# Cross-attention on one core: both blocks of scores in one run, the output product one round later, second-stage pieces behind the projections

## The reference, cut to what matters

```python
# layer 0, attention: 8 heads of 64, keys and values from the context (77 rows) and from the tokens themselves
xn, cn = layer_norm(x, ln_x_w, ln_x_b), layer_norm(ctx, ln_l_w, ln_l_b)
q = xn @ Wq
k, v = split(concat(xn, cn) @ Wkv)
q, k = l2norm(q) * q_scale, l2norm(k) * k_scale
p = softmax(8.0 * q @ k.T + mask)
x = x + layer_norm((p @ v) @ Wo, ln_o_w, ln_o_b)
# layer 0, feed-forward: a quantised product; layer 1: attention through We and W2, then one expert of 8 per token
```

## Time and profile before

| | |
|---|---|
| three timed runs | 951.37, 953.4, 954.11 us; median 953.4 |
| profiled execution, its own time | the profile gives its span, 950.6 us, and no other figure |
| TensorE busy | 912.8 us (96% of the span) |
| VectorE busy | 744.9 us (78%) |
| ScalarE busy | 693.5 us (73%) |
| GpSimd busy | 458.1 us (48%) |
| TensorE's granted clock, mean | 0.997 |
| most time on the chain that ended last | TensorE 69%, VectorE 14%, ScalarE 8% |

### The profile page before, as it was taken

One profiled execution on the slowest core, in us unless ns is written; L12 is line 12 of the kernel. 1 busy time (PEld: TensorE's weight loads), 2 busy tenths in 40 slices (PEclk: granted clock), 3 DMA queues, 4 the chain that ended last, 5 costly groups with the idle time before them and its releaser, 6 DMA issues.

```text
span 950.6 us, 30821 instructions
## 1 busy us (share of the span) xinstructions
PE 912.8 (96%) x11286; PEld 794.5 (84%) x11286; DVE 744.9 (78%) x2526; ACT 693.5 (73%) x1671; POOL 458.1 (48%) x1094
## 2 busy tenths in 40 slices
PE   7999999999999999999999999999999999899997
PEld 6788888788878887888788878888888878898997
DVE  5566787888888888888888888888888978877553
ACT  4877777677778787778777777777778766676664
POOL 5422433354535453545354444444454545777554
PEclk9999999999999999999999999999999999999999
DMA  7743000000000000000000000000000022245310
GB/s 196 200 124 57 2 2 2 2 13 2 14 2 14 2 14 2 13 3 10 5 10 5 8 8 8 7 8 7 8 8 8 7 47 71 61 97 106 95 55 20
DMA packets 45193, 31.44 MB, mean 33 GB/s; under 512 B 11555, under 2 KB 40166, under 8 KB 45046
## 3 DMA queue, kind: packets, MB, share of 16 engines
q1 hardware_dynamic: 39398, 19.93, 9.2%
q0 software_dynamic: 4320, 8.50, 2.8%
q10 hardware_dynamic: 1328, 1.06, 0.4%
HBM read 17.75 MB, written 12.17 MB: 31 GB/s over the span
## 4 chain that ended last, share of the span: by engine, by line
PE 69%; DVE 14%; ACT 8%; issue 3%; POOL 3%; DMA 1%; SPq 1%; DVEq 0%; POOLq 0%; ACTq 0%
PE ps L1670 9%; PE ps L1717 9%; PE ps L1643 7%; PE ps L1765 6%; PE ps L1450 5%; PE ps L1622 5%; PE ps L1630 5%; PE ps L1452 5%; PE ps L1451 5%; DVE sumsq L1267 4%; PE ps L1722 3%; ACT probs L604 2%; PE ps L1749 2%; ACT qk_hat L617 2%; PE ps L1496 1%
## 5 line engine op out<-in xcount | busy, mean ns | idle before, releaser
L1374 DVE TENSOR_TENSOR qk_hat<-ps,rstd 128x512 f32<-128x512 f32 x168 | 106.3, 684 | 49.2 <-POOL rstd L870 49.1
L1267 DVE TENSOR_REDUCE sumsq<-qk_hat 128x8 f32<-128x512 f32 x168 | 107.8, 677 | 35.9 <-ACT qk_hat L617 34.7
L863 POOL TENSOR_TENSOR rs_t<-rs_y 128x32 f32<-128x32 f32 x73 | 17.9, 245 | 235.2 <-ACT rs_y L658 235.2
L1670 PE MATMUL ps<-v_x,prob 128*64 128x65 f32 x2048 | 127.9, 225 | 2.1 <-ACT w_all L568 0.4
L1670 PE MATMUL ps<-v_c,prob 128*64 128x65 f32 x2048 | 124.2, 222 | 0.0
L677 ACT ACTIVATE prob<-ps,neg_shift 128x512 f32<-128x512 f32 x128 | 88.4, 690 | 48.6 <-PE ps L1717 48.6
L1670 PEld LDWEIGHTS ps<-v_x,prob 128*64 128x64 f32 x2048 | 105.0, 137 | 20.9 <-issue 19.2
L617 ACT ACTIVATE qk_hat<-ps 128x512 f32<-128x512 f32 x168 | 98.5, 599 | 31.7 <-PE ps L1452 25.8
L1450 PE MATMUL ps<-w_hi,xc_hi 128*128 128x512 f32 x272 | 120.8, 444 | 0.8 <-POOL xc_lo L835 0.8
L1717 PE MATMUL ps<-qT_all,kT_all 64*128 64x128 f32 x1536 | 111.6, 285 | 2.3 <-ACT prob L677 1.1
L1452 PE MATMUL ps<-w_hi,xc_lo 128*128 128x512 f32 x272 | 107.3, 395 | 0.0
(11 more groups left out here) (245 smaller groups left out, 2257.2 us busy)
## 6 DMA issues: line engine op xcount, KB each, us to landing
x_res<-sorted_rows SPq DMA_DIRECT2D x71, 65.5 KB, 1.9
w_all<-in_L_ffn_W_dram SPq DMA_DIRECT2D x16, 256.0 KB, 5.3
sorted_rows<-fill SPq DMA_DIRECT2D x8, 327.5 KB
out_dram<-prob,x_res POOLq DMA_INDIRECT x71
sorted_rows<-stage,idx POOLq DMA_INDIRECT x64, 2.4
ctx_res<-in_ctx_dram SPq DMA_DIRECT2D x8, 115.5 KB
x_res<-in_x_dram SPq DMA_DIRECT2D x1, 768.0 KB
sorted_rows<-fill SPq DMA_DIRECT2D x1, 524.0 KB, 5.0
```

The lines of the kernel that those rows point to most:

```text
L1267: nc.vector.reduce_sum(sumsq[:, n * H:(n + 1) * H], sq[:, n * INNER:(n + 1) * INNER].rearrange("p (h d) -> p h d", d=DH), AX).then_inc(ss_ ...
L1374: nc.vector.tensor_tensor(qk_hat[:, n * INNER:(n + 1) * INNER].rearrange("p (h d) -> p h d", d=DH), ps_qk[:, n, :].rearrange("p (h d) -> p ...
L1670: last = nc.tensor.matmul(dst[half:half + DH, :], prob[:, kt, col + half:col + half + DH], v, start=kt == 0, stop=kt == 1)
```

## The change

The numbers of instructions and their shapes stay as they are. The two blocks of scores follow one another directly; the second waits for on_done, since quarters 2 and 3 now use banks 4 and 3. The transposed output goes to bank 6 and waits for the exp that reads it. The output product of batch j - 2 stands behind the first transposes of round j, and waits for o_t. slot_a waits for the first three exps. In rounds of rho 1, 2 and 3 slot_b stands behind the query and key products, and the quantised transposes behind all of them. In slot_c of rho 0 the transposes of t_b stand ahead of the rank matmuls. ScalarE does exps 0 and 1, the scaled tokens, exp 3, o_t, exp 2, and copies the quantised transposes after all squares. VectorE takes the statistics of the next tokens ahead of those of ps_o; the reciprocal of the second stage's sums ahead of the sums of squares; `places` behind them; and `later` behind o_n.

```diff
-        ps_v, ps_ot = (ps[:, 6, :], ps[:, 5, :]), ps[:, 3, :]
-        ps_s = (ps[:, 6, :], ps[:, 5, :], ps[:, 4, :], ps[:, 6, :])
+        ps_v = (ps[:, 6, :], ps[:, 5, :])
+        ps_s = (ps[:, 6, :], ps[:, 5, :], ps[:, 4, :], ps[:, 3, :])
...
+        def output_bank(j, inside):
+
+            return ps[:, 6, :] if has(j, inside) else ps[:, 3, :]
...
-                        if n == 0:
-                            quantised_copied()
+                    quantised_copied()
...
-                if has(j, inside):
-                    exps((0,))
                 if not inside and j == 0:
                     second_weights(j)
+                if has(j, inside):
+                    exps((0, 1))
                 if inside or j != -2:
                     scaled_tokens()
+                if has(j, inside):
+                    exps((3,))
                 if has(j - 1, inside) and not tail(j, inside):
                     outputs_copied()
                 if has(j, inside):
-                    exps((1, 3, 2))
+                    exps((2,))
...
+            def sums_inverted(j, rho, g, inside):
+                if rho == 1 and group(g - 1, inside):
+
+                    after(dve, "pr_done", g - 1, inside)
+                    nc.vector.reciprocal(sinv[0:M, :], ssum[0:M, :]).then_inc(s["sinv_done"], 1)
...
-                if has(j - 2, inside):
-                    dve.wait_ge(wo_done, j - 1)
-                    nc.vector.bn_stats(o6[:, :], ps_o).then_inc(o_bn, 1)
-                    dve.wait_ge(o_bn, j - 1)
-
...
                 if has(j - 2, inside):
+                    dve.wait_ge(wo_done, j - 1)
+                    nc.vector.bn_stats(o6[:, :], ps_o).then_inc(o_bn, 1)
...
                 if not tail(j, inside):
-                    places(j, rho, g, inside)
+                    sums_inverted(j, rho, g, inside)
                 if not inside and TOTAL_AT <= j < TAIL:
                     first_table(j, 0)
                 if has(j + 1, inside) and (inside or j != -1):
                     sums_of_squares(j, pos)
-
                 if not tail(j, inside):
-                    later(j, par, rho, g, inside)
+                    places(j, rho, g, inside)
...
+                if not tail(j, inside):
+                    later(j, par, rho, g, inside)
...
             def slot_a(j, rho, g, inside):
 
+                if has(j - 1, inside):
+                    pe.wait_ge(exp_done, 4 * j - 1)
...
+            def outputs(b, inside):
+
+                pe.wait_ge(ot_done, b + 1)
+                if has(b + 3, inside):
+                    pe.wait_ge(xct_sb, b + 4)
+                elif has(b - 1, inside):
+                    pe.wait_ge(o_cent, b)
+                for t in range(PAIRS):
+                    last = nc.tensor.matmul(ps_o, o_t[:, t * P:(t + 1) * P], wo_sb[:, t, :],
+                                            start=t == 0, stop=t == PAIRS - 1)
+                last.then_inc(wo_done, 1)
...
+                if has(j - 2, inside) and (inside or j <= B):
+                    outputs(j - 2, inside)
                 slot_a(j, rho, g, inside)
...
-                slot_b(j, rho, g, inside)
+                between = rho == 0 or not has(j + 1, inside)
+                if between:
+                    slot_b(j, rho, g, inside)
...
-                        if n == 0:
-                            quantised(j, rho, g, inside)
-                else:
-                    quantised(j, rho, g, inside)
+                quantised(j, rho, g, inside)
+                if not between:
+                    slot_b(j, rho, g, inside)
                 slot_c(j, rho, g, inside)
...
                     scores(0)
+                    if has(j - 1, inside):
+                        pe.wait_ge(on_done, j)
...
+                    scores(1)
...
                     pe.wait_ge(on_done, j)
+                    if has(j, inside):
+                        pe.wait_ge(exp_done, 4 * j + 1)
...
-                if has(j, inside):
-
-                    pe.wait_ge(exp_done, 4 * j + 1)
-                    if halves(pos)[0] != halves(pos)[1]:
-                        pe.sem_inc(s["fence_t"], 1)
-                    scores(1)
-                if has(j - 1, inside):
-
-                    pe.wait_ge(ot_done, j)
-                    if not has(j + 2, inside) and has(j - 2, inside):
-                        pe.wait_ge(o_cent, j - 1)
-                    if has(j + 2, inside):
-                        pe.wait_ge(xct_sb, j + 3)
-                    for t in range(PAIRS):
-                        last = nc.tensor.matmul(ps_o, o_t[:, t * P:(t + 1) * P], wo_sb[:, t, :],
-                                                start=t == 0, stop=t == PAIRS - 1)
-                    last.then_inc(wo_done, 1)
+                if has(j - 1, inside) and not has(j, inside):
+                    outputs(j - 1, inside)
```

## The result

The changed kernel takes 956.8 us (median of 6 runs, 954.6 to 959.0) against 953.0 us (median of 6, 951.4 to 954.1): a ratio of 1.0041 with a 95% interval of 1.0027 to 1.0056. It is slower by 0.4%. The prediction said 946.9 us and faster; the time lies inside its range of 935 to 958, on the wrong side of the kernel before.

The account below looks back on a forecast made before the run. TensorE was taken as the clock. Scores to slot +0.86 us and slot to scores -1.85 made -1.0 us per eight-round period, -6.5 us over 6.5 periods: 946.9 us from a median of 953.4, range 935 to 958.

Parts of the forecast that it names:

- B: Round with two token blocks transposed, two tiles next; first score matmul to first matmul after next transposes: 5.08 to 5.50 us.
- Part 1: Joining both score blocks on TensorE saves tile changes: about 0.38 us a round, half that in four rounds a period.
- Part 2: Second score block waits for o_n, starting 1.11 us after the scores began; restarting costs 0.06 us.
- Part 3: Output product waits for o_t, late in ScalarE's queue: TensorE stands 0.8 us in B, 0.37 in C.
- A: Round with one token block transposed, three tiles next; scores to slot forecast 5.04 us, from 5.32 (-0.28).
- C: Round with two token blocks transposed, three tiles next; scores to slot forecast 5.50 us, from 5.43 (+0.07).
- Part 4: Transposes at L1643 come 1.3 us earlier; qk_hat mostly ready, D gains 0.31 us, one round a period loses 0.6.
- D: Round with one token block, three tiles and a late o_n; scores to slot forecast 5.28 us, from 5.59 (-0.31).
- Part 5: Slot to scores, the rest of a round: moved pieces cover waits for o_c, onehot and tc_t, -1.85 us a period.
- Drains that pay in full: Rival: o_t comes early, so all saved tile-change drains count: 918 us, halfway about 932; chance 0.15 for both.
- Nothing lands: Rival: TensorE reaches the scores earlier but waits the same time for qk_hat, period unchanged: 953 us; chance 0.14.
- VectorE's head: Rival: late statistics of ps_o at VectorE's start of the round delay everything behind, 0.3 us a round: 960 us; chance 0.16.

Follow-up runs that it names:

- e1: The changed kernel with one swap in ScalarE's queue, o_t copied ahead of the exp of quarter 3: 941.0 us.
- e8: The changed kernel without joined scores (banks, waits and exps' order as before); later output product, moved pieces and statistics' order stay: 939.1 us.
- e4: The changed kernel with places alone moved back ahead of the sums of squares on VectorE: 952.5 us.
- e3: The kernel before with only the second-stage pieces moved as in the change, on TensorE, ScalarE and VectorE: 937.2 us.
- e2: The changed kernel with the second-stage pieces back at their old places; joined scores and later output product stay: 973.8 us.
- e9: The changed kernel with o_t copied ahead of the exp of quarter 3 and places ahead of the sums of squares: 939.9 us.
- e10: The kernel before with the second-stage pieces moved and places ahead of the sums of squares: 932.0 us.
- e11: e9 with the token transposes, and their wait for bank 7, between the two blocks of scores: 936.8 us.
- e7: The changed kernel with later (and the table's second pieces) behind the scaled tokens and the residual on VectorE: 967.3 us.
- e12: e8 with VectorE's statistics of ps_o at the head of the round, waiting there for the later output product: 949.3 us.

## Why the prediction was wrong

**Its sign turned on sizes, added over a period.** The mechanism, waits for o_n and o_t that give the drains back, was named rightly. The step that failed is the sum of the first part, scores to slot: 0.86 us a period was forecast and 1.81 measured, 0.67 of the difference in the three B rounds (1.26 forecast, 1.93 measured). Two smaller steps failed beside it: the prediction had nobody waiting for place, and rounds 59 to 62 were counted as rounds like the others. Of its parts:

*Part 1* was right in its price of a change of tile, and there is no break between the blocks but the one of part 2.

*Part 2* placed the second block at 1.11 us after the first; the record of 2.27 us agrees. The term that was too small is the restart. I took 0.06 us from transposes, since the block stays in one mode. It is 0.10 us, as on a change of mode, for scores and for the output product (the first records after a wait are 373 and 377 ns long, as at a drain). With two stalls in most rounds that is an estimated 0.08 us a round.

*Part 3* named the wait that gave the gain back, and its mechanism is shown by e1 (15.8 us from one swap) and e8 (17.7 us without the joined scores). Its sum was too small: A 5.14 (5.04 predicted), B 5.73, 5.63 and 5.63 (5.50), C 5.60 twice (5.50). In the first B a mode entry for L1501 was left out. The "before" of B was also taken from one round, 5.08; the other two stood at 4.99, which hides another 0.18 us a period. (The round of the earlier trace rows errs the other way: it stood at 5.42, not at A's 5.32.) In all the first part grew by 1.81 us, not 0.86. With 0.86 the period would still have come out shorter.

*Part 4* held: D 5.32 (5.28), the round of the earlier trace rows 5.69 (5.64).

*Part 5* gained 1.62 us, not 1.85. The wait at L1539 went (7.24 to 6.12 in that round), that at tc_t too (6.47 to 6.11). The new wait for place made one round of rho 0 0.28 us longer (6.11 to 6.39) and took most of the gain in the other (6.64 to 6.51, and 6.16 in e4). I had counted places among what "fills the wait for rstd" and not asked who waits for it: TensorE's three_emptied does. e4 prices it at 4.3 us.

*The sum* then is +0.2 us a period, about +1.6 us from round 12 to 59. Rounds 59 to 62, which the prediction counted as half a period, cost 2.5 us. In round 59 qk_hat starts no later than before, 3.01 us after the scores (736.98 - 733.97) where it was 3.08 (733.45 - 730.37). But before, the product filled that time, and now it stands behind the transposes that wait, L1669, for 0.76 us. The timeline of that round, first of the kernel before, then of the kernel after, VectorE's line last in each:

```profile
730.37 1.16 PE L1717 MATMUL ps<-qT_all,kT_all 64*128 64x128 f32 x16
...
733.64 1.16 PE L1765 MATMUL ps<-wo_sb,o_t 128*128 128x128 f32 x8
...
733.45 1.88 DVE L1374 TENSOR_TENSOR qk_hat<-ps,rstd 128x512 f32<-128x512 f32 x3 [0.55 <-POOL rstd L870]
```

```profile
733.97 1.16 PE L1746 MATMUL ps<-qT_all,kT_all 64*128 64x128 f32 x16
...
737.72 1.85 PE L1669 MATMUL ps<-ident,qk_hat 128*128 128x128 f32 x12 [0.76 <-DVE qk_hat L1386]
739.41 1.06 PE L1659 MATMUL ps<-wo_sb,o_t 128*128 128x128 f32 x8
...
736.98 1.89 DVE L1386 TENSOR_TENSOR qk_hat<-ps,rstd 128x512 f32<-128x512 f32 x3
```

The last column of the table bears this out. e3 has the moved pieces, later behind o_n among them, with the product at its old place, and loses nothing there (48.2). e2 has the pieces at their old places and the later product (50.5), e8 the later product without joined scores (50.4). The loss goes with the later product and its order of the statistics. Part 4 knew this mechanism and applied it to D and to the round of the earlier trace rows only.

The first twelve rounds, put at zero, cost another 0.55 us, and the rounds and tiles from 63 on give back 0.7. The first slot comes 1.36 us later in this execution, while over the profiles of this study it comes at 22.7 to 25.1 us, with early and late ones among joined scores and among scores apart; I put that down to the loads at the start, without a test.

*The rivals.* Drains that pay in full are refuted: e9 and e10 differ by the joined scores and the later product, with the banks, the exps' order and the statistics' order that belong to them, and the joined one is 7.9 us slower; e11 adds drains and gets faster. The rule of the Trainium skill, "TensorEngine Tiling (Array Packing)", section "Key Properties", that a change of mode drains the engine, agrees with the records (373 against 272 ns). What a drain is worth where the engine would wait otherwise is seen in e9 and e11 alone. "Nothing lands" (953) is refuted by e3, where the pieces' gains landed. "VectorE's head", at 960, was nearest in sign and size, but by another mechanism: e8 has the same later product and statistics and, by its ratio, takes no longer than e3. Only in round 37 and in rounds 59 to 62 does that half cost something, and e7 and e12 show how near the head lay.

What stays open is how e9's 7.9 us over e10 divide. 2.5 us of them fall into rounds 59 to 62 (50.1 against 47.6), where the later product accounts for a like loss without joined scores. Of the rest, 0.75 us a period, no run takes apart the wait for o_n with its restart and qk_hat met too early; the second appears in the waits (15.7 us in e9 against 1.2 in e10).

## What to carry to other kernels

When a saved overhead brings an engine to its next operand sooner, write down what that operand's own queue does next, for every kind of round; the gain is only what reaches past the wait, and a small net of two large sums has no sign until each is right to a tenth. Move a piece to a place where something waits anyway, and ask of each piece who waits for it: the same microsecond of VectorE work cost nothing under the wait for rstd and 10 to 16 us in all at the head of the next round. The same holds for work that is itself a filler: the output product ahead of the late transposes filled a wait, and behind them it adds to it. Test the halves of a change apart: here one was worth -16 us and the other +21.

## What the runs showed of the hardware

A stalled matmul pays the price of entering a mode even where the mode stays: after a wait the first score records are 373 ns against 272 and the next pair comes 0.21 us later in place of 0.11. The view of the line in the kernel after (least, median, most, ns):

```profile
L1746 PE MATMUL ps<-qT_all,kT_all x1536: 272/272/373, 29.7 to 784.2; 64*128 64x128 f32 x192
...
L1659 PE MATMUL ps<-wo_sb,o_t x512: 275/275/377, 45.4 to 796.1; 128*128 128x128 f32 x171
```

The product at L1659 follows transposes in its own mode (128x128). Record by record, its first one is 377 ns long and the next starts 0.21 us later in the 47 rounds in which it had to wait; in 16 rounds it found o_t ready, and there it is 275 ns and 0.11 us. In e8, where the product waits for o_t in the first and last rounds at most, it is 275 ns in 62 rounds of 64. So the length goes with the stall. For a transpose after a stall or a change of tile the first record is 329 ns where it is else 273. Beside a wait much of the price of a drain is thus paid already, which fits e11, where more drains cost nothing; no run isolates it.
